# Row maxima ahead of the attention loop: 22 tiles from the difference of the two halves of the keys, and the maxima's first way through DRAM put ahead of other transfers

## The reference, cut to what matters

```
q = (x @ W_Q.T).reshape(B, S, 16, HEADS);  k, v likewise with KV = HEADS // 2 heads
q, k = compute_rope(q), compute_rope(k)
scores = einsum('bsdkg,btdk->bkgst', q, k) / sqrt(256)
w = softmax(scores, axis=-1)
ctx = einsum('bkgst,btdk->bkgsd', w, v)
```

## Time and profile before

| | |
|---|---|
| device time, median of 3 runs | 884.34 us |
| the three runs | 884.34, 892.65, 880.03 us |
| span of the profiled execution | 864.7 us |
| device time of the profiled execution | not shown beside its span |
| mean granted clock of TensorE | 0.945 |
| busy: TensorE, VectorE, ScalarE, GpSimd | 780.4, 694.2, 524.5, 363.9 us |
| largest group of VectorE | L695, 256 reductions, 297.7 us, 1213 ns each |

### The profile page before, as it was taken

How to read it: one execution, slowest core, us unless ns; L and a number is a source line. 1 busy time by engine, 2 the same in 40 slices (tenths; PEclk the granted TensorE clock), 3 DMA queues, 4 the chain that set the end, 5 groups by cost and what they waited for, 6 DMA issues and landing times. The chain is left out here.

```text
span 864.7 us, 17911 instructions
## 1 busy us (share of the span) xinstructions
PE 780.4 (90%) x6593; PEld 503.9 (58%) x6593; DVE 694.2 (80%) x1094; ACT 524.5 (61%) x965; POOL 363.9 (42%) x296
## 2 busy tenths in 40 slices
PE   3999999999999999998999999899575989999996
PEld 2863333333333333332368888798465887999875
DVE  5789999999999999996137666567899877666586
ACT  4520688888788888886864333543757653666442
POOL 6430255535753575359410001003698680444340
PEclk9985799999999999997999999999587989999999
DMA  6497022222222222200029000000104423344352
GB/s 240 174 225 290 2 46 54 52 52 52 52 53 52 52 52 52 56 16 13 20 85 250 2 1 0 14 1 13 60 5 150 174 93 60 117 131 127 115 160 74
DMA packets 59510, 69.97 MB, mean 81 GB/s; under 512 B 24768, under 2 KB 46400, under 8 KB 59040
## 3 DMA queue, kind: packets, MB, share of 16 engines
q1 hardware_dynamic: 55272, 58.30, 24.9%
q0 software_dynamic: 3408, 9.38, 3.1%
q10 hardware_dynamic: 744, 1.15, 0.4%
HBM read 40.07 MB, written 26.62 MB: 77 GB/s over the span
## 5 line engine op out<-in xcount | busy, mean ns | idle before, releaser
L681 ACT ACTIVATE probs_t<-psum 128x512 f32<-128x512 f32 x512 | 271.6, 601 | 98.7 <-PE psum L781 96.7
L695 DVE TENSOR_REDUCE row_max<-psum 128x1 f32<-128x1024 f32 x256 | 297.7, 1213 | 6.2 <-PE psum L765 5.9
L622 POOL TENSOR_TENSOR lut_sum<-lut_sum,lut_tmp 128x1080 f32<-128x1080 f32 x60 | 151.8, 2530 | 160.6 <-DVE lut_tmp L720 159.9
L765 PE MATMUL psum<-KS,QS 48*128 48x512 f32 x512 | 188.7, 470 | 19.6 <-DVE row_max L695 18.6
L781 PE MATMUL psum<-QS,KS 50*128 50x512 f32 x512 | 194.7, 471 | 1.0 <-ACT probs_t L681 1.0
L781 PEld LDWEIGHTS psum<-QS,KS 50*128 50x128 f32 x512 | 82.9, 189 | 135.3 <-ACT probs_t L681 124.7
L793 PE MATMUL psum<-probs_t,VS 128*32 128x512 f32 x1024 | 139.1, 616 | 1.0
L765 PEld LDWEIGHTS psum<-KS,QS 48*128 48x128 f32 x512 | 81.3, 199 | 76.1 <-DVE row_max L695 70.9
L2420 POOL DMA_INDIRECT y_rows<-y_slot,ids x39 | 37.5, 961 | 62.4 <-ACT y_slot L2483 62.1
L720 DVE TENSOR_SCALAR lut_tmp<-lut_idx,lut 128x1080 f32<-128x1080 int32 x60 | 48.7, 813 | 10.2 <-POOL lut_sum L622 10.2
L1179 POOL TENSOR_TENSOR rstd<-var_eps,minus_half 128x4 f32<-128x4 f32 x8 | 8.4, 1044 | 100.5 <-DVE var_eps L1174 100.5
(11 more groups left out here) (322 smaller groups left out, 1801.9 us busy)
## 6 DMA issues: line engine op xcount, KB each, us to landing
KS<-k_rows SPq DMA_DIRECT2D x31, 192.0 KB, 4.6
QS<-q_rows SPq DMA_DIRECT2D x31, 192.0 KB, 4.9
x_rows<-zero_rows SPq DMA_DIRECT2D x1, 4992.0 KB, 17.8
x_slot<-x_rows SPq DMA_DIRECT2D x39, 128.0 KB, 2.2
m_raw<-experts_w SPq DMA_DIRECT2D x2, 2432.0 KB, 13.3
q_rows<-part SPq DMA_DIRECT2D x8, 512.0 KB, 8.7
y_token<-y_rows SPq DMA_DIRECT2D x8, 512.0 KB, 7.6
x_tok<-x SPq DMA_DIRECT2D x4, 512.0 KB, 7.4
```

What stands on the lines that cost most here:

```text
L622: nc.gpsimd.tensor_tensor(wsum[:, c % 2, :], wsum[:, c % 2, :], wtmp[:, slot % 2, :], ALU.add).then_inc(lut_add, 1)
L681: nc.scalar.activation(pt[:, k % NPT, :], ring(k)[:], ACT.Exp, scale=float(E) ** -0.5).then_inc(p_ready, 1)
L695: nc.vector.tensor_reduce(mx[:, n % 2, col:col + 1], m.psum[:, 2 * (k % 2):2 * (k % 2) + 2, :], AX_XY, ALU.max).then_inc(max_done, 1)
L765: mm = nc.tensor.matmul(MX[k % 2][h][:], QS[n % NQK][rows(g, NROW), st * P:(st + 1) * P], KS[n % NQK][rows(g, NROW), h * BLK:(h + 1) * BLK ...
```

## The change

For the tiles 4 to 25 (the last 12 of group 0 and the first ten of group 1) the matmul of h 0 no longer multiplies by the first half of the keys but by the difference of the halves, KD. The row maximum over both halves is the maximum over 512 pairs of b + relu(a - b), where b is the second half's score: ScalarE takes the relu of the difference from PSUM into SBUF, and VectorE adds the other bank and takes the maximum in one instruction (tensor_tensor_reduce). Tiles 0 to 3 and all from 26 on are as before. The first 26 tiles use all eight banks in four pairs, and wait for the tile four before.

The difference of the rotated keys of the blocks 0 and 1 is computed on GpSimd, cut into high part (ScalarE) and low part (GpSimd), written to DRAM as kd_rows (two transfers), and read back for groups 0 and 1 into KD (two loads each). In the sync engine's queue the order is now: blocks 0 and 1 out, kd_rows out, half of group 0, group 1, KD 1, group 2, lut and the first table, place_max(0), group 3, blocks 2 and 3 out, place_max(1), the wait for the blocks. The second table goes into round 1. The look-up sums get a buffer of their full length, so that look_up doesn't wait for f_lo.

```diff
+    def difference(pool):
+        pool.wait_ge(rot_ready, 6)
+        nc.gpsimd.tensor_tensor(kd[:], krot[0][:], krot[1][:], ALU.subtract).then_inc(kd_ready, 1)
+    def difference_high(act):
+        act.wait_ge(kd_ready, 1)
+        nc.scalar.activation(kdh[:], kd[:], ACT.Copy).then_inc(kd_hi, 1)
+    def difference_low(pool):
+        pool.wait_ge(kd_hi, 1)
+        nc.gpsimd.tensor_tensor(kdl[:], kd[:], kdh[:], ALU.subtract).then_inc(kd_lo, 1)
+    def difference_out(sp):
+        sp.wait_ge(kd_hi, 1)
+        sp.wait_ge(kd_lo, 1)
+        for i, src in ((HI, kdh), (LO, kdl)):
+            dst = m.kd_rows[:, K_AT[i], :]
+            sp.dma_start(dst, src[:].bitcast(F32).unsqueeze(1).broadcast_to([P, dst.shape[1], BLK])).then_inc(kd_out, 16)
     def rope(dve, tb):
...
+        if tb >= NB // 2:
+            dve.wait_ge(kd_ready, 1)
+        nc.vector.tensor_tensor(krot[tb % 2][:], prod[:, 4, :], prod[:, 5, :], ALU.add).then_inc(rot_ready, 1)
     def project_scalar(act):
...
         take_xt(3)
+        difference_high(act)
...
         cut(act, 2)
+        act.wait_ge(kd_out, 32)
+        m.load_diff(act, 0)
         take_v(act, 2)
     def project_gpsimd(pool):
...
             low_parts(pool, tb)
+            if tb == 1:
+                difference(pool)
+                difference_low(pool)
+    FIRST, PLAIN = NST + AHEAD, 4
+    def pair(k):
+        return 2 * (k % 4) if k < FIRST else 2 * (k % 2)
+    def by_relu(k):
+        return PLAIN <= k < FIRST
+    def load_diff(queue, n):
+        for g in range(G):
+            queue.dma_start(KD[n][g * HEAD_ROWS:g * HEAD_ROWS + NROW, :].bitcast(F32),
+                            m.kd_rows[n * HD:(n + 1) * HD, :, :].rearrange("r s t -> (r s) t")).then_inc(kd_in[n], 16)
     def attend_sync(sp):
...
+        m.difference_out(sp)
         load_qk(sp, 0, (0,))
-        for n in range(1, NQK):
-            load_qk(sp, n)
-        for tb in range(NB // 2, NB):
-            m.block_out(sp, tb)
-        for i in range(2):
-            sp.wait_ge(m.part_out[i], 16 * m.OUTS * NB // 2)
+        load_qk(sp, 1)
+        sp.wait_ge(m.kd_out, 32)
+        load_diff(sp, 1)
+        load_qk(sp, 2)
         sp.dma_start(lut[:], ...)
         sp.dma_start(idx[:, 0:KC * GUW], ...)
-        sp.dma_start(idx[:, KC * GUW:], ...)
+        place_max(sp, 0)
+        load_qk(sp, NQK - 1)
+        for tb in range(NB // 2, NB):
+            m.block_out(sp, tb)
         for n in range(NG):
+            if n == 0:
+                place_max(sp, 1)
+                for i in range(2):
+                    sp.wait_ge(m.part_out[i], 16 * m.OUTS * NB // 2)
             if n >= 1:
                 ...
                 leave(sp, n - 1)
-            if n + 1 < NG:
+            if n == 1:
+                sp.wait_ge(max_done, 2 * NST)
+                sp.dma_start(idx[:, KC * GUW:], ...)
+            if 1 <= n < NG - 1:
                 place_max(sp, n + 1)
+    def part_above(act, k):
+        act.wait_ge(max_ps, k + 1)
+        if k == PLAIN:
+            act.wait_ge(m.prod_k, 2 * NB)
+        nc.scalar.activation(relus[k % 4][:], bank[pair(k)], ACT.Relu).then_inc(relu_done, 1)
     def attend_scalar(act):
         m.project_scalar(act)
-        place_max(act, 0)
+        for k in range(PLAIN, FIRST):
+            part_above(act, k)
     def row_max(n, i):
...
+            if by_relu(k):
+                dve.wait_ge(relu_done, k - PLAIN + 1)
+                above = relus[k % 4]
+                nc.vector.tensor_tensor_reduce(above[:], bank[j + 1], above[:], 1.0, LOWEST, ALU.add, ALU.max,
+                                               out).then_inc(max_done, 1)
+            else:
+                nc.vector.tensor_reduce(out, m.psum[:, j:j + 2, :], AX_XY, ALU.max).then_inc(max_done, 1)
     def maximum(k, h):
...
-            if k >= 2 and h == 0:
-                pe.wait_ge(max_done, k - 1)
+            back = 4 if k < FIRST else 2
+            if k >= back and h == 0:
+                pe.wait_ge(max_done, k - back + 1)
...
+            if by_relu(k) and h == 0:
+                pe.wait_ge(kd_in[n], 16 * G)
+                keys = KD[n][rows(g, NROW), :]
```

More of the change, by code:

```diff
@@ L484, in attention_stage @@
     idx = at("lut_idx", [P, NLUT], I32, b)
+    down_at = b + KC * GUW * 4
+    m.fh = at("ffn_h", [P, NLUT], F32R, b); b += NLUT * 4
+    wsum_at = b
+    wsum = at("lut_sum", [P, NLUT], F32, b)
     m.fl = at("ffn_l", [P, NLUT], F32R, b); b += NLUT * 4
-    m.fh = at("ffn_h", [P, NLUT], F32R, b); b += NLUT * 4
     m.woh = at("wo_h", [P, KC, E], F32R, b); b += KC * E * 4
@@ L489, in attention_stage @@
     m.w1 = b
-    wsum = at("lut_sum", [P, 2, PIECE], F32, b); b += 2 * PIECE * 4
-    lut = at("lut", [P, LUT], F32, b); b += LUT * 4
+    KD = [at(f"KD{i}", [P, BLK], F32R, down_at + i * BLK * 4) for i in range(2)]
+    lut = at("lut", [P, LUT], F32, m.probs_end + 2 * BLK * 4)
     assert b <= m.qk_at, b
+    relus = [at(f"relu{i}", [P, BLK], F32, o) for i, o in enumerate(
+        (m.probs_end, down_at + 2 * BLK * 4, wsum_at, wsum_at + BLK * 4))]
+    assert m.probs_end + 2 * BLK * 4 + LUT * 4 <= m.p0 + 34304 and wsum_at + 2 * BLK * 4 <= m.part_at
     lut_in, idx_in, lut_prod, lut_add, f_hi, f_lo = (
@@ L503, in attention_stage @@
     mres_done = sem("mres_done")
+    relu_done = m.front_sem("relu_done")
+    kd_in = [m.front_sem(f"kd_in{i}") for i in range(2)]
     gu_ps = m.gu_ps = sem("gu_ps")
@@ L694, in row_max @@
             col = i % G * NTT + i // G
-            nc.vector.tensor_reduce(mx[:, n % 2, col:col + 1], m.psum[:, 2 * (k % 2):2 * (k % 2) + 2, :],
-                                    AX_XY, ALU.max).then_inc(max_done, 1)
+            out, j = mx[:, n % 2, col:col + 1], pair(k)
+            if by_relu(k):
[5 more added lines that the diff above has]
+                nc.vector.tensor_reduce(out, m.psum[:, j:j + 2, :], AX_XY, ALU.max).then_inc(max_done, 1)
         def turn_max(n):
@@ L712, in look_up @@
                 dve.wait_ge(lut_in, 16)
+                dve.wait_ge(idx_in, 16)
+                dve.wait_ge(max_done, FIRST)
+            if (c + 1) * PIECE > KC * GUW and v == 0:
                 dve.wait_ge(idx_in, 32)
@@ L758, in maximum @@
                 pe.wait_ge(qk_in[n % NQK], 16 * m.LOADS * (n // NQK + 1))
-            if k >= 2 and h == 0:
-                pe.wait_ge(max_done, k - 1)
+            back = 4 if k < FIRST else 2
+            if k >= back and h == 0:
+                pe.wait_ge(max_done, k - back + 1)
             if k == 1 and h == 0:
                 pe.wait_ge(m.v_out, NT)
+            if k == 2 and h == 0:
+                pe.wait_ge(m.prod_q, 4 * NB)
+                pe.wait_ge(m.prod_k, 2 * NB)
             st, g = divmod(i, G)
-            mm = nc.tensor.matmul(MX[k % 2][h][:], QS[n % NQK][rows(g, NROW), st * P:(st + 1) * P],
-                                  KS[n % NQK][rows(g, NROW), h * BLK:(h + 1) * BLK], start=True, stop=True)
+            keys = KS[n % NQK][rows(g, NROW), h * BLK:(h + 1) * BLK]
+            if by_relu(k) and h == 0:
+                pe.wait_ge(kd_in[n], 16 * G)
+                keys = KD[n][rows(g, NROW), :]
+            mm = nc.tensor.matmul(bank[pair(k) + h], QS[n % NQK][rows(g, NROW), st * P:(st + 1) * P], keys,
+                                  start=True, stop=True)
             if h == 1:
@@ L774, in scores @@
                 pe.wait_ge(m_in, 16 * G * (n + 1))
-            if n == 0 and t == 0 and i == 0:
-                pe.wait_ge(m.prod_q, 4 * NB)
-                pe.wait_ge(m.prod_k, 2 * NB)
             if k >= 3:
@@ L817, in up_two @@
                 mm.then_inc(gu_ps, 1)
-        for k in range(NST + AHEAD):
+        for k in range(FIRST):
             maximum(k, 0)
```

43 lines of the change are left out of this document (26 added, 17 removed).

## The result

The changed kernel took 872.53 us (median of 4 runs, 870.93 to 873.95); the kernel before, run beside it on the same chip, 882.88 (880.03 to 892.65, 4 runs). The ratio is 0.9891 [0.9858, 0.9925], 9.6 us less. The brackets hold a 95% interval; the 9.6 us are the ratio's, the two medians lie 10.35 apart. Two later comparisons gave 0.9894 [0.9856, 0.9931] and 0.9911 [0.9878, 0.9944]. So the change makes the kernel faster, by 1%. 874.1 had been forecast.

A forecast was written before the change was run, and what follows sets the result against it. VectorE was taken to bound the loop, and its queue of 26 tiles the front: 11.3 less 1.0 gives 10.2 us off the loop's start, so 884.34 becomes 874.1 us. Range 868 to 884, own range 870 to 878.

The forecast's parts named there:

- The direction and the sum: Start of the attention loop: 11.3 us less from tiles, 1.0 lost to arrivals, so 10.2 us less in all.
- Theory A: Experiments' opening theory: the front is a chain of tiles, arrival and hop; what it loses in length comes off the time.
- Fused tile: VectorE's tiles 4 to 25 ahead of the loop: 0.73 us each instead of 1.27, 11.3 us less over 21.
- Rival 2: Fused instruction on VectorE runs at half rate, 1.32 us a tile: 2 us slower, 886 us; chance 0.09.
- Arrival of the difference rows: Read-back before tile 4: rows land by 55 to 60, needed at 58.9; 1.0 us lost together with the first loads.
- The hop of group 0: Group 0's maxima through DRAM before the first score: 2.78 us between issues instead of 6.39, landing near 77, no loss.
- Rival 1: Sync queue near 95 us: writes of blocks 2 and 3 delay group 1's hop, up to 4.4 us, 878; chance 0.15.
- Rival 3: TensorE's clock comes back by the loop's start: 1.0 us more, another 1.0 without arrival delay, 872 us; chance 0.10.
- Rival 4: Front shortens, but the clock falls elsewhere or GpSimd's table sums bind; half the gain lost, 879 us; chance 0.08.
- which VectorE, bound to 99.6%, carries through: Attention loop: the 10.2 us off its start stay won to the end, since VectorE sets the loop's pace.
- the prediction's last sign: Attention loop: the forecast is wrong in kind if VectorE has gaps between 80 and 390 us.
- The profiled span: Whole kernel: median 884.34 us lies 19.6 above the 864.7 us span, and the same 10.2 come off it.

The follow-up runs named there:

- b0: The kernel before, unchanged, run for one more profile; 878.28 us, one run.
- a0: The changed kernel again, nothing altered; 874.98 us, ratio 0.9894 to the kernel before.
- a2: The changed kernel a third time, nothing altered, beside e9; 860.97 us, ratio 0.9911 to the kernel before.
- e3: Changed kernel with the difference rows read back ahead of the loads of groups 1 and 2; 871.43 us, ratio 0.9844 to the kernel before.
- e2: Changed kernel with eight plain tiles instead of four ahead of the fused ones; 873.58 us, ratio 0.9894 to the kernel before.
- e8: The kernel of e3 again, beside the changed kernel; 873.35 us, ratio 0.9877 to the kernel before.
- e5: Changed kernel with each matmul of tiles 4 to 25 issued twice; 881.25 us, ratio 0.9963 to the kernel before.
- e6: e3 with one more 128-row matmul, its result unused, in each fused tile; 891.96 us, ratio 1.0129 to the kernel before.
- e9: e3 with three plain tiles and group 1's hop between the writes of blocks 2 and 3; 856.13 us, ratio 0.9854 to the kernel before.

## Why the prediction was right, step by step

- **The direction and the sum.** Forecast 10.2 us less, from the start of the loop; measured 9.6, 9.4 and 7.7 us in three comparisons (1 minus the ratio, times the median of before there). They sit on the front, which shortened by 31.57 - 22.99 = 8.6 us, or 8.2 by b0 and a0; the microsecond between 8.6 and 9.6 is within the interval and is given no cause. Theory A holds for the size of it: e1 undid the fused tiles and lost most of the gain, e4 put the hop behind the writes and lost all.
- **Fused tile.** Forecast 0.73 us, measured 0.685: the instruction 0.69 with starts 0.61 apart, as the product in the earlier trace rows. The read of the accumulator costs nothing of its own, because it lies beside the next instruction; the rest is the 0.21 at each fourth tile and the start after it. 21 tiles and the transpose: 14.44 us (64.89 to 79.33), forecast 15.53. Off by 1.1 in the good direction. Rival 2, half rate, is refuted by these rows. The Trainium skill's sentence (Vector Engine (DVE) Microarchitecture Reference, section "Points that are easy to get wrong") is on two non-bf16 sources in SBUF, for an instruction that it calls S2S2D2_STT. With one source in PSUM this change lies outside it, and the trace agrees: 0.69 us, not 1.2. No run here has the fused form with both sources in SBUF.
- **Arrival of the difference rows: the mis-sized term.** Forecast 1.0 us for everything that has to arrive; measured 3.86 on VectorE in the first profile, 4.44 and 4.95 in a0 and a2. The prediction took the middle of a landing of 3.2 to 8.2 us, for data written by 52. The loads were indeed issued at 52.07, but they landed 8.7 to 10.3 us later, outside the range, because group 1's loads were ahead of them and group 2's beside. e3 took those away and the wait was zero; e2 covered it with four tiles. The step that failed is "the middle of either landing is early enough": the low end was read in a quiet queue, and this load was not put in one. The trace of before already had the nearer price: KS loads issued from 48.5 to 56 us, behind others, landed 7.0 to 11.3 us after their issue, median 9.3. Its first half, the first loads, was right: 56.41 against 56.12.
- **Together.** 61.03 (end of the plain tiles) + 3.86 + 14.44 = 79.33, forecast 60.73 + 1.0 + 15.53 = 77.3. The two errors, and 0.3 us at the first reduction, leave 2.1 us; that they partly cancel is luck.
- **The hop of group 0.** Forecast 2.78 between its issues, measured 2.76, and in SBUF before it was needed. Right. e4 shows what a bad place costs: behind the writes the hop takes 9.44, and the whole gain goes. The forecast's own bound, 3.2 us with the hop of before, was not tested.
- **Rival 1, group 1's hop.** Forecast an arrival by 97 and 3 us to spare, no stall; measured an issue at 96.66, so an arrival near 98.5 by the estimate above, and some 5 us to spare, because group 4's load came at 103.84 and not at 100.0. No stall is right, but with help from the late loop start: e3 and e8 started 2 us sooner than the forecast, and e8 stood 0.36 us for this hop.
- **Rival 3, the clock early.** It did not come back in the front in any of the kernels, e5 and e6 with their full TensorE among them.
- **Rival 4, the shift given back.** The forecast step "which VectorE, bound to 99.6%, carries through" and its 22.7 us from first score to group 4's load came from one profile. That stretch measured 22.6 us in before, 25.6 in b0, 24.4, 22.8 and 22.8 in the three of after, 25.9 in e9: it goes with the clock's return, 9 to 19 us after the first score matmul. And the clock fell at a new place in two of three profiles of the changed kernel. That is rival 4's mechanism. Its price is the line above, 0.34 to 0.38 us per microsecond at 1.2 GHz, at most 10 us between the best loop and the worst. It did not take half of the gain here. e8's front is 4.3 us shorter than a0's beside it and its median only 1.6 us lower. In the two profiled executions e8's loop takes 1.2 us of the 4.3 back, and their times lie 3.4 us apart; the rest of the difference is within the spread of the runs. By the prediction's last sign, VectorE has gaps between 80 and 390 us: 3.6 us in all from 79.4 to 94.4 here, but 4.0 from 86.7 to 105.7 in b0 too. VectorE binds the loop only from where the clock is back.
- **The profiled span.** The 19.6 us "around the span" were a mistake in reading. It did no harm, because the sum was a difference. What made that execution of before short lies behind the attention: from 577.27 to 711.67, two table loads of ScalarE, 134.4 us, against 145.7 in b0 and 145.2 in after. In the comparison of a2 and e9, where all kernels were 14 to 15 us faster, it was 134.9 and 135.2. What makes this stage short or long was not found.

Not settled: what makes the clock fall at 210 us in one execution and not in another; whether e9's gain of 4.5 us over the changed kernel are its shorter front (5.3 us) in full, or partly luck of the clock. Its profile is 2.6 us below that of a2, its loop 2.0 longer.

## What to carry over

When a new load is put into a queue, price its landing from rows of loads that had as much issued just ahead of them, and not from the middle between quiet and loaded ones; if the data is needed first, issue it first. Work and a round trip through DRAM that run side by side have to be shortened together: without the faster tiles some 2.7 us were left of 9, with the hop behind the writes 0. And before a difference of a few microseconds in a long loop is explained by its code, look at the time at the low clock in it.

## What the runs showed that I had not expected

- In all 14 profiles the clock came back 9 to 19 us after the first score matmul, with TensorE busy 4.00 of 4 us for most of it; 16 us of doubled 48-row matmuls (e5) and 38 us with 128-row ones among them (e6, from 57.4 on) did not bring it back.
- A 128-row matmul overlapped with no 48-row neighbour (starts 0.55 and 0.73 us apart, 1.87 a tile), while two 48-row ones in different row groups run side by side.
- Reading VectorE's accumulator back, 0.08 us, cost no time between two fused instructions.
- A 96 KB load took 8.7 to 10.3 us to land with 768 KB of loads issued just ahead of it, and 3.5 to 4.6 without them (e3).
